# One core, gated-expert feed-forward on fp32 split in two: a bias load, one weight sum and one weight rest stand elsewhere in their queues

## The chip, the cores and the metric

One core of a Trainium2 chip. The metric is the device time of one execution in microseconds (us); 943.2 us is the median of three runs of the kernel before. One execution was also profiled, and all rows below come from it. 0.2% of the time is 1.9 us.

## The reference

```python
W = weights[condition]                      # one of 16 tables (64 x 64) for each of 128 batches
z = einsum('bct,bcd->bdt', x, W)
result = z @ W_base.T + b_base
logits = z @ W_gate.T                       # 8 experts
top_p, top_i = top_k(softmax(logits), 2)    # scaled to sum 1
h  = einsum('bnd,erd->bner', z, A)          # rank 16 for each of 8 experts
hw = h * route_w
out = x + result + einsum('bner,eor->bno', hw, B)
```

x has 128 batches of 64 rows and 1024 columns, so 8192 rows of 1024 fp32 values; all weights are fp32.

## The kernel before, in words

The order of the two linear maps is turned round: x is first multiplied by all weights (W_base, A and W_gate side by side, 1160 columns), which gives z; then `mix_chunk` (L829) multiplies z by the table of the batch. Every fp32 operand is split in two parts, hi (a copy rounded by ScalarE, functions `..._top`) and lo (whole minus hi, by VectorE or GpSimd, functions `..._rest`), and each product is three matmuls: hi·hi, hi·lo, lo·hi.

The 8192 rows are 64 tiles of 128, taken as 32 pairs of tiles, a and b (t = 0 and 1). The 1160 columns are three chunks: L (312 of W_base, the 128 of A, the 8 of W_gate: 448), Q (448) and R (264). From the third pair on, chunks L and Q of a pair are done by Strassen's scheme in seven products instead of eight. It needs sums of the weight blocks: T1 to T4, made once in `t_sum` (L614, VectorE), cut by `t_top` (L432, ScalarE) and `t_rest` (L618, VectorE). It also needs sums S1 to S4 of the halves of x^T, made for each pair by GpSimd (`sum_s1` to `sum_s4`, L322 to L347). The first pair and the second pair (function `first` of each engine, p = 1) are done with the weight blocks B11, B21, B12 and B22 themselves (`first_q`, L865), while the T's are made.

For each tile the rest goes: z is split (`z_top`, `z_rest`), mixed into banks ps_out that ScalarE has filled with the bias (`seed`, L443); from chunk L VectorE ranks the experts (`rank_experts`, L655), ScalarE takes one exponential (`exps`), VectorE makes hw (`weigh_experts`, L670). TensorE transposes hw (`turn_hw`, L838), hw is split (`hwt_top`, `hwt_rest`, L645) and multiplied by B (`lora`, L842) onto ps_out. VectorE adds x and the bank (`output`, L649), and SyncE's queue stores it.

The order on each engine is written out by hand, and semaphores tie the engines together. Four places matter here:

- SyncE's queue (from L218) issues the loads: x^T and weights in the order of need. `load_w` (L222) loads a weight block in two halves of 448 KB. The bias rows follow (L261 to L263), broadcast to 128 partitions. ScalarE copies the halves of B22 (`w_top`, L428) and then waits for all three bias loads before it seeds the banks.
- VectorE makes T1 and T3 right before its `first`, and T2 and T4 in it (L719 to L737), between work for tile b of the first pair (`hwt_rest(1)`, `output(0, 1, c)`) and tile a of the second.
- GpSimd in `first` (L382): it fetches the mixing tables (`fetch_mix`), makes S3 and S1 of the third pair, two a_lo (`a_rest`), then S2 and S4.
- TensorE's `first` (L949): `lora(1, c)` waits for hwt_lo; then mixing and lora of tile a; it ends with a wait for all four T rests (L982).

The queue of VectorE around the sums:

```python
            weigh_experts(0, 1)
            t_sum(1, T1, T3, T1)
            t_sum(3, T3, T2, T3)
            def first():
                z_rest(1, 0, L, ps_1[:, 0:NS])
                hwt_rest(1)
                t_sum(2, T2, T2, T1)
```

Of the kernel before, what the change touches and what calls it, by code (L numbers as in the profile page):

```python
# [13 lines left out]
P = 128  # L14
BANK = 512

BASE_COLS = [312, 448, 264]

L, Q, R = 0, 1, 2

B11, B21, B22, NT4, T1, T2, T3 = range(7)
# [9 lines left out]
def adaln_ffn(nc, x, x_t, cond, cond_w, w_t, b_t, b_base, out):  # L31
# [26 lines left out]
    at = [sum(width[:c]) for c in range(3)]  # L58
# [6 lines left out]
    with ExitStack() as ctx:  # L65
        def sb(name, shape, dt=F32):
            return ctx.enter_context(nc.sbuf_tensor(name, shape, dt))
# [10 lines left out]
        def sem(name):  # L78
            return ctx.enter_context(nc.semaphore(name))
# [10 lines left out]
        bias = sb("bias", [P, COLS])  # L90
# [43 lines left out]
        s_bias_in = sem("bias_in")  # L134
# [15 lines left out]
        s_w0_lo = {g: sem(f"{g}_lo_made") for g in ("B11", "B21", "B12", "B22")}  # L150
# [46 lines left out]
        def cols(c):  # L197
            return slice(at[c], at[c] + width[c])

        def base(c):  # L200
            return slice(base_at[c], base_at[c] + BASE_COLS[c])

        def ks(h):
            return slice(2 * h, 2 * h + 2)

        def as_f32(tile):
            return tile.bitcast(F32)

        def pairs(engine, first, step):
            first()  # L210
            with engine.Fori(2, PAIRS - 1) as p:
                step(p, False)
            step(PAIRS - 1, True)
# [3 lines left out]
        @block.sync  # L217
        def _(sp):  # L218
            w_src = w_t.rearrange("(k p) n -> p k n", p=P)
            home = {"B11": (T1, 0, L), "B21": (NT4, 1, L), "B12": (T3, 0, Q), "B22": (T2, 1, Q)}  # L220

            def load_w(g):  # L222
                at_g, half, c = home[g]
                for h in range(2):
                    sp.dma_start(w_sum[:, at_g, ks(h), :],
                                 w_src[:, half * KH + 2 * h:half * KH + 2 * h + 2, cols(c)]).then_inc(s_w_in[g][h], 16)

            def load_r(j):
                sp.dma_start(r_raw[:, ks(j), :], w_src[:, ks(j), cols(R)]).then_inc(s_r_in[j], 16)

            def load_raw(p, j):
                tile, half = 2 * p + j // 2, j % 2
                src = x_t[tile] if isinstance(tile, int) else \
                    x_t[bass.ds(tile, 1)].rearrange("a p k r -> (a p) k r")
                sp.dma_start(raw[j][:], src[:, half * KH:(half + 1) * KH, :]).then_inc(s_raw_in[j], 16)

            def load_x(p, t):
                sp.dma_start(o_sb[t][:], x[bass.ds((2 * p + t) * P, P), :]).then_inc(s_x_in[t], 16)

            def store(p, t):  # L240
                sp.wait_ge(s_out[t][(Q, R)[t]], p + 1)
                sp.dma_start(out[bass.ds((2 * p + t) * P, P), :], o_sb[t][:]).then_inc(s_stored[t], 16)

            load_raw(0, A11)
            load_r(0)
            load_raw(0, A21)
            load_r(1)
            load_w("B11")
            load_raw(0, A12)
            load_raw(0, A22)  # L250
            load_r(2)
            load_r(3)
            load_w("B21")
            for b in range(2):
                sp.dma_start(table_raw[b * C:(b + 1) * C], cond_w).then_inc(s_table_in, 16)
            load_w("B12")
            load_w("B22")
            for j in (A11, A21, A22):
                sp.wait_ge(s_a_lo[j], 1)
                load_raw(1, j)  # L260
            for c in range(3):  # L261
                sp.dma_start(bias[:, at[c]:at[c] + BASE_COLS[c]],
                             b_base[:, base(c)].to_broadcast([P, BASE_COLS[c]])).then_inc(s_bias_in, 16)  # L263
            sp.dma_start(b_raw[:], b_t).then_inc(s_b_in, 16)
            load_x(0, 0)
            sp.wait_ge(s_a_lo[A12], 1)
            load_raw(1, A12)
            load_x(0, 1)

            def step(p, last, first=False):  # L270
                if first:
                    sp.wait_ge(s_a_lo[A11], 2)
                elif not last:
                    sp.wait_ge(s_s_sum[2], p - 1)
                if not last:
                    load_raw(p + 1, A11)
                store(p - 1, 0)
                if not last:
                    sp.wait_ge(s_a_lo[A21], p + 1)
                    load_raw(p + 1, A21)  # L280
                    sp.wait_ge(s_a_lo[A22], p + 1)
                    load_raw(p + 1, A22)
                sp.wait_ge(s_stored[0], 16 * p)
                load_x(p, 0)
                if first:
                    sp.wait_ge(s_a_lo[A12], 2)
                elif not last:
                    sp.wait_ge(s_s_lo[4], p - 1)
                if not last:
                    load_raw(p + 1, A12)  # L290
                store(p - 1, 1)
                sp.wait_ge(s_stored[1], 16 * p)
                load_x(p, 1)

            pairs(sp, lambda: step(1, False, True), step)
            for t, c in ((0, L), (0, R), (0, Q), (1, L), (1, Q), (1, R)):
                sp.wait_ge(s_out[t][c], PAIRS)
                sp.dma_start(out[(TILES - 2 + t) * P:(TILES - 1 + t) * P, base(c)], o_sb[t][:, base(c)])\
                    .then_inc(s_stored[t], 16)
            sp.wait_ge(s_stored[0], 16 * (PAIRS + 2))  # L300
            sp.wait_ge(s_stored[1], 16 * (PAIRS + 2))
# [294 lines left out]
        def _(dve):  # L596
# [17 lines left out]
            def t_sum(t, to, one_at, other_at):  # L614
                dve.tensor_tensor(w_sum[:, to], w_sum[:, one_at], w_sum[:, other_at],  # L615
                                  ALU.subtract).then_inc(s_t_sum[t], 1)

            def t_rest(t, at_g):  # L618
                dve.wait_ge(s_t_hi[t], 1)
                dve.tensor_tensor(w_lo[:, at_g], w_sum[:, at_g], as_f32(w_hi[:, at_g]),  # L620
                                  ALU.subtract).then_inc(s_t_lo[t], 1)
# [23 lines left out]
            def hwt_rest(i, whole=ps_hwt[:, 0:P]):  # L645
                dve.wait_ge(s_hwt_hi, i + 1)
                dve.tensor_tensor(hwt_lo[:], whole, as_f32(hwt_hi[:]), ALU.subtract).then_inc(s_hwt_lo, 1)

            def output(p, t, c, bank=None):  # L649
                dve.wait_ge(s_x_in[t], 16 * p + 16)  # L650
                dve.wait_ge(s_out_mm[t][c], p + 1)
                dve.tensor_tensor(o_sb[t][:, base(c)], (bank or ps_out[c])[:, 0:BASE_COLS[c]], o_sb[t][:, base(c)],  # L652
                                  ALU.add).then_inc(s_out[t][c], 1)
# [65 lines left out]
            weigh_experts(0, 1)  # L719
            dve.wait_ge(s_w0_lo["B11"], 2)  # L720
            t_sum(1, T1, T3, T1)
            dve.wait_ge(s_w0_lo["B12"], 2)
            t_sum(3, T3, T2, T3)

            def first():
                z_rest(1, 0, L, ps_1[:, 0:NS])
                hwt_rest(1)
                dve.wait_ge(s_t_sum[1], 1)
                dve.wait_ge(s_t_sum[3], 1)
                dve.wait_ge(s_w0_lo["B22"], 2)  # L730
                t_sum(2, T2, T2, T1)
                for c in (L, Q, R):
                    output(0, 1, c)
                dve.wait_ge(s_t_sum[2], 1)
                dve.wait_ge(s_w0_lo["B21"], 2)
                t_sum(4, NT4, NT4, T2)
                rank_experts(1, 0)  # L737
                weigh_experts(1, 0)
                t_rest(1, T1)
                z_rest(1, 0, Q, ps_6[:, 0:NS])  # L740
                dve.wait_ge(s_t_sum[4], 1)
                t_rest(2, T2)
                z_rest(1, 0, R, ps_r[:, 0:width[R]])
                hwt_rest(2)
                dve.wait_ge(s_t_sum[3], 1)
                t_rest(3, T3)
                z_rest(1, 1, Q, ps_5[:, 0:NS])
                for c in (L, R, Q):
                    output(1, 0, c)
                t_rest(4, NT4)  # L750
                z_rest(1, 1, L, ps_1[:, 0:NS])
                z_rest(1, 1, R, ps_r[:, 0:width[R]])
                rank_experts(1, 1)
                weigh_experts(1, 1)
                turn_hw(3)
# [38 lines left out]
            def finish(p):  # L794
# [10 lines left out]
                output(p, 1, R)  # L805

            pairs(dve, first, step)

        @block.tensor
# [259 lines left out]
```

## Time and profile before

| | before |
|---|---|
| median of 3 runs (lowest to highest) | 943.2 us (943.04 to 944.24) |
| the profiled execution's own time | 942.72 us |
| its span (first to last instruction) | 941.0 us |
| TensorE matmuls busy | 935.8 us, 99% |
| VectorE busy | 525.5 us, 56% |
| GpSimd busy | 535.8 us, 57% |
| ScalarE busy | 384.4 us, 41% |
| granted TensorE clock | full in all slices |
| DMA, mean of the span | 114 GB/s |

The 1.7 us between own time and span lie outside the recorded instructions. A busy share is an average; which wait ends last at a place is read from the timeline there. Matmul rows of the timeline overlap: a matmul of 448 columns is listed with 0.36 us, and the next one starts 0.20 us after it. Missing time on TensorE is thus seen in the distance between starts.

### The profile page before, as it was taken

What the parts mean: (1) busy time and instruction counts of PE and PEld (TensorE: products, weight loads), DVE (VectorE), ACT (ScalarE), POOL (GpSimd) and SP (SyncE); (2) the same over time, 40 slices, a digit from 0 to 9 for tenths busy, and PEclk for the clock granted to TensorE, in tenths of its full rate; (3) what the DMA queues carried; (4) which work ended last, traced back from release to release, by engine and by line L of the source; (5) the groups of instructions that cost most, each with busy time, mean ns of one, the idle gap of its engine ahead of it and who ended that gap; (6) DMA issues with size and microseconds to landing.
All of it is one profiled execution on the core that took longest, in us unless ns stands there. A gap on an engine that the chain in (4) does not pass through costs nothing.

```text
span 941.0 us, 17296 instructions
## 1 busy us (share of the span) xinstructions
PE 935.8 (99%) x5444; PEld 880.9 (94%) x5444; DVE 525.5 (56%) x1808; ACT 384.4 (41%) x810; POOL 535.8 (57%) x506
## 2 busy tenths in 40 slices
PE   9999999999999999999999999999999999999998
PEld 7899999999999999999999999999999999999997
DVE  5785555545555455555555554555555555555554
ACT  6463343434334334444334344333443343434332
POOL 3575546655566555575555665555655547555560
PEclk9999999999999999999999999999999999999999
DMA  9522332233322233322333223333223332233312
GB/s 306 187 79 101 134 115 98 89 111 123 134 92 92 95 123 134 111 99 91 108 126 127 95 86 104 123 134 105 87 89 120 134 112 100 89 111 123 134 45 90
DMA packets 41453, 107.13 MB, mean 114 GB/s; under 512 B 4450, under 2 KB 8675, under 8 KB 41443
## 3 DMA queue, kind: packets, MB, share of 16 engines
q1 hardware_dynamic: 41440, 107.01, 32.9%
q8 instruction: 5, 0.08, 0.0%
q14 instruction: 6, 0.04, 0.0%
q10 hardware_dynamic: 2, 0.00, 0.0%
HBM read 73.43 MB, written 33.55 MB: 114 GB/s over the span
## 4 chain that ended last, share of the span: by engine, by line
PE 98%; DVE 1%; DMA 0%; ACT 0%; issue 0%; SPq 0%; DVEq 0%
PE ps L816 54%; PE ps_r L816 19%; PE ps_out L834 11%; PE ps_out L844 10%; PE ps L875 2%; PE ps L886 1%; DVE w_sum L615 1%; PE ps_r L875 1%; DMA raw<-in_x_t 0%; PE ps_hwt L840 0%; ACT a_hi L418 0%; PE ps_r L861 0%; PE ps L861 0%; PE ps L834 0%; DVE o_sb L652 0%; PE ps L844 0%
## 5 line engine op out<-in xcount | busy, mean ns | idle before, releaser
L316 POOL TENSOR_TENSOR a_lo<-raw,a_hi 128x512 fp32r<-128x512 f32 x128 | 165.9, 1318 | 245.1 <-ACT a_hi L418 245.1
L816 PE MATMUL ps<-w_hi,s_hi 128*128 128x448 f32 x480 | 177.6, 370 | 0.0
L816 PE MATMUL ps<-w_lo,s_hi 128*128 128x448 f32 x480 | 175.5, 366 | 0.0
L816 PE MATMUL ps<-w_hi,s_lo 128*128 128x448 f32 x480 | 173.6, 362 | 0.0
L632 DVE TENSOR_TENSOR z_sum<-ps,z_sum 128x448 f32<-128x448 f32 x150 | 93.7, 625 | 128.5 <-PE ps L816 128.3
L816 PE MATMUL ps_r<-r_hi,a_hi 128*128 128x264 f32 x496 | 140.7, 284 | 0.0
L816 PE MATMUL ps_r<-r_hi,a_lo 128*128 128x264 f32 x496 | 140.7, 284 | 0.0
L816 PE MATMUL ps_r<-r_lo,a_hi 128*128 128x264 f32 x496 | 140.6, 284 | 0.0
L652 DVE TENSOR_TENSOR o_sb<-ps_out,o_sb 128x312 f32<-128x312 f32 (+1 forms) x190 | 93.1, 505 | 76.8 <-PE ps_out L844 76.7
L816 PE MATMUL ps<-w_hi,a_hi 128*128 128x448 f32 x360 | 131.9, 367 | 0.0
L816 PE MATMUL ps<-w_hi,a_lo 128*128 128x448 f32 x360 | 130.6, 363 | 0.0
L816 PE MATMUL ps<-w_lo,a_hi 128*128 128x448 f32 x360 | 130.3, 362 | 0.0
L320 POOL TENSOR_TENSOR s_lo<-s_sum,s_hi 128x512 fp32r<-128x512 f32 x90 | 126.3, 1419 | 0.0
L834 PE MATMUL ps_out<-z_hi,mix 128*128 128x448 f32 (+1 forms) x380 | 120.9, 338 | 0.0
L446 ACT COPY ps_out<-bias 128x448 f32<-128x448 f32 (+1 forms) x190 | 90.0, 487 | 60.4 <-DVE o_sb L652 57.8
L642 DVE STREAM_TRANSPOSE hwt_sum<-hw 32x32 f32<-32x32 f32 x480 | 97.5, 203 | 15.1
L422 ACT CAST s_hi<-s_sum 128x512 fp32r<-128x512 f32 x90 | 55.7, 620 | 105.7 <-POOL s_sum L341 93.1
L816 PEld LDWEIGHTS ps<-w_hi,s_hi 128*128 128x128 f32 x480 | 90.0, 187 | 8.8
L816 PEld LDWEIGHTS ps<-w_hi,s_lo 128*128 128x128 f32 x480 | 90.0, 188 | 7.4
L816 PEld LDWEIGHTS ps<-w_lo,s_hi 128*128 128x128 f32 x480 | 90.2, 188 | 5.2
L816 PEld LDWEIGHTS ps_r<-r_lo,a_hi 128*128 128x128 f32 x496 | 93.4, 188 | 0.5
L816 PEld LDWEIGHTS ps_r<-r_hi,a_hi 128*128 128x128 f32 x496 | 93.2, 188 | 0.5
(135 smaller groups left out, 1711.3 us busy)
## 6 DMA issues: line engine op xcount, KB each, us to landing
raw<-in_x_t SPq DMA_DIRECT2D x128, 256.0 KB, 2.7
o_sb<-in_x SPq DMA_DIRECT2D x64, 512.0 KB, 3.6
out_x<-o_sb SPq DMA_DIRECT2D x62, 512.0 KB, 2.6
w_sum<-in_w_t SPq DMA_DIRECT2D x8, 448.0 KB, 9.2
r_raw<-in_w_t SPq DMA_DIRECT2D x4, 264.0 KB, 5.7
table_raw<-in_cond_w SPq DMA_DIRECT2D x2, 256.0 KB, 8.8
b_raw<-in_b_t SPq DMA_DIRECT2D x1, 512.0 KB, 10.8
out_x<-o_sb SPq DMA_DIRECT2D x2, 224.0 KB, 2.1
```

The costliest lines, as they stand in the source:

```text
L316: pool.tensor_tensor(a_lo[j][:], raw[j][:], as_f32(a_hi[j][:]), ALU.subtract).then_inc(s_a_lo[j], 1)
L320: pool.tensor_tensor(lo[:], whole, as_f32(hi[:]), ALU.subtract).then_inc(s_s_lo[j], 1)
L422: act.copy(hi[:], whole).then_inc(s_s_hi[j], 1)
L446: act.copy(ps_out[c][:, 0:width[c]], bias[:, cols(c)]).then_inc(s_seed[c], 1)
L615: dve.tensor_tensor(w_sum[:, to], w_sum[:, one_at], w_sum[:, other_at], ALU.subtract).then_inc(s_t_sum[t], 1)
L632: return dve.tensor_tensor(to, bank[:, 0:NS], other, ALU.add)
L642: dve.transpose(hwt_sum[c * TURN:(c + 1) * TURN, r * TURN:(r + 1) * TURN], hw[r * TURN:(r + 1) * TURN, c * TURN:(c + 1) * TURN]).then_inc( ...
L652: dve.tensor_tensor(o_sb[t][:, base(c)], (bank or ps_out[c])[:, 0:BASE_COLS[c]], o_sb[t][:, base(c)], ALU.add).then_inc(s_out[t][c], 1)
L816: mm = pe.matmul(bank[:, 0:w.shape[-1]], a[:, k, :], w[:, k, :], start=(opens and k == 0 and q == 0), stop=(closes and k == KH - 1 and q = ...
L834: mm = pe.matmul((bank or ps_out[c])[:, 0:width[c]], mix[t][:, m, :], z[t][:, cols(c)], start=False, stop=(q == 2), skip_group_check=True)
L844: mm = pe.matmul((bank or ps_out[c])[:, 0:BASE_COLS[c]], h[:], b[:, base(c)], start=False, stop=(q == 2), skip_group_check=True)
L875: mm = pe.matmul(bank[:, 0:NS], u[a][:, k, :], v[:, k, :], start=(half == 0 and k == 0 and q == 0), stop=(half == 1 and k == KH - 1 and q ...
```

## The change

SyncE's queue issues the three bias loads before the two loads of B22, not after them and the three loads of x^T. On VectorE the sum of T3 moves from in front of tile a's z_lo and tile b's hwt_lo to behind them; the three outputs of tile b now come before the sum of T2, and the rest of T1 is made after tile a's z_lo of chunks Q and R and its hwt_lo. Nothing is added or removed.

```diff
             load_w("B12")
+            for c in range(3):
+                sp.dma_start(bias[:, at[c]:at[c] + BASE_COLS[c]],
+                             b_base[:, base(c)].to_broadcast([P, BASE_COLS[c]])).then_inc(s_bias_in, 16)
             load_w("B22")
             for j in (A11, A21, A22):
                 sp.wait_ge(s_a_lo[j], 1)
                 load_raw(1, j)
-            for c in range(3):
-                sp.dma_start(bias[:, at[c]:at[c] + BASE_COLS[c]],
-                             b_base[:, base(c)].to_broadcast([P, BASE_COLS[c]])).then_inc(s_bias_in, 16)
@@
             t_sum(1, T1, T3, T1)
-            dve.wait_ge(s_w0_lo["B12"], 2)
-            t_sum(3, T3, T2, T3)
 
             def first():
                 z_rest(1, 0, L, ps_1[:, 0:NS])
                 hwt_rest(1)
+                dve.wait_ge(s_w0_lo["B12"], 2)
+                t_sum(3, T3, T2, T3)
+                for c in (L, Q, R):
+                    output(0, 1, c)
                 dve.wait_ge(s_t_sum[1], 1)
                 dve.wait_ge(s_t_sum[3], 1)
                 dve.wait_ge(s_w0_lo["B22"], 2)
                 t_sum(2, T2, T2, T1)
-                for c in (L, Q, R):
-                    output(0, 1, c)
                 dve.wait_ge(s_t_sum[2], 1)
                 dve.wait_ge(s_w0_lo["B21"], 2)
                 t_sum(4, NT4, NT4, T2)
                 rank_experts(1, 0)
                 weigh_experts(1, 0)
-                t_rest(1, T1)
                 z_rest(1, 0, Q, ps_6[:, 0:NS])
                 dve.wait_ge(s_t_sum[4], 1)
                 t_rest(2, T2)
                 z_rest(1, 0, R, ps_r[:, 0:width[R]])
                 hwt_rest(2)
+                t_rest(1, T1)
                 dve.wait_ge(s_t_sum[3], 1)
                 t_rest(3, T3)
                 z_rest(1, 1, Q, ps_5[:, 0:NS])
```

The queue of SyncE in the loads ahead of the first pair, as a difference (in_b_base is the bias, in_w_t the weights, raw the halves of x^T):

```order
 L255 DMA table_raw<-in_cond_w 64x1024 x2
-L225 DMA w_sum<-in_w_t 128x2x448 x4
+L225 DMA w_sum<-in_w_t 128x2x448 x2
+L258 DMA bias<-in_b_base 128x312
+L258 DMA bias<-in_b_base 128x448
+L258 DMA bias<-in_b_base 128x264
+L225 DMA w_sum<-in_w_t 128x2x448 x2
 L235 DMA raw<-in_x_t 128x512 x3
```

The bias stands between B12 and B22, ahead of two weight loads and three loads of x^T that it stood behind.

VectorE from tile b's hw of the first pair to the expert ranks of the second pair's tile a; L615 is a T sum, L625 a z_lo, L652 an output:

```order
 L682 SCALAR_TENSOR_TENSOR hw<-h_sb,e_inv,ps_hwt 128x128
-L615 TENSOR_TENSOR w_sum<-w_sum 128x1792 x2
+L615 TENSOR_TENSOR w_sum<-w_sum 128x1792
 L625 TENSOR_TENSOR z_lo<-ps,z_hi 128x448
 L647 TENSOR_TENSOR hwt_lo<-ps_hwt,hwt_hi 128x128
```

```order
 L652 TENSOR_TENSOR o_sb<-ps_out,o_sb 128x264
-L615 TENSOR_TENSOR w_sum<-w_sum 128x1792
+L615 TENSOR_TENSOR w_sum<-w_sum 128x1792 x2
 L659 COPY h_sb<-ps_out 128x64
```

One sum instead of two stands in front of z_lo and hwt_lo, one (T3) between hwt_lo and the outputs, and two (T2 and T4) in a row in front of the ranks.

VectorE behind tile a's hw; L620 is a T rest:

```order
 L682 SCALAR_TENSOR_TENSOR hw<-h_sb,e_inv,ps_hwt 128x128
-L620 TENSOR_TENSOR w_lo<-w_sum,w_hi 128x1792
 L625 TENSOR_TENSOR z_lo<-ps,z_hi 128x448
 L620 TENSOR_TENSOR w_lo<-w_sum,w_hi 128x1792
 L625 TENSOR_TENSOR z_lo<-ps_r,z_hi 128x264
 L647 TENSOR_TENSOR hwt_lo<-ps_hwt,hwt_hi 128x128
-L620 TENSOR_TENSOR w_lo<-w_sum,w_hi 128x1792
+L620 TENSOR_TENSOR w_lo<-w_sum,w_hi 128x1792 x2
 L625 TENSOR_TENSOR z_lo<-ps,z_hi 128x448
```

The z_lo of chunk Q follows hw at once, and two T rests (T1 and T3) now stand in a row behind hwt_lo.

## Rows read from the trace of the kernel before

**Rows 1.** The page, the chain that ended last, shares by engine.
```profile
PE 98%; DVE 1%; DMA 0%; ACT 0%; issue 0%; SPq 0%; DVEq 0%
```
**Rows 2.** Waits of PEld, whole span: line, waited for, total us, times, longest us.
```profile
PEld ps_out L834 <- issue: 0.4, 1, 0.4
PEld ps_out L834 <- DVE z_lo L625: 0.3, 1, 0.3
```
**Rows 3.** Timeline of PE at the first mixing: start, us, engine, line, op, out<-in, count.
```profile
26.89 0.37 PE L875 MATMUL ps_r<-w_hi,a_lo 128*128 128x448 f32 x1
27.29 0.44 PE L834 MATMUL ps_out<-z_hi,mix 128*128 128x448 f32 x1
```
**Rows 4.** Timeline of ACT; the idle time before and its releaser in brackets.
```profile
23.02 0.95 ACT L430 CAST w_hi<-w_sum 128x896 fp32r<-128x896 f32 x1
26.61 1.32 ACT L446 COPY ps_out<-bias 128x448 f32<-128x448 f32 x3 [2.64 <-DMA bias<-in_b_base]
...
41.95 0.53 ACT L437 CAST z_hi<-ps 128x448 fp32r<-128x448 f32 x1 [3.90 <-PE ps L875]
...
66.11 0.52 ACT L437 CAST z_hi<-ps 128x448 fp32r<-128x448 f32 x1
```
**Rows 5.** Issues of B22 on SP, their time to landing, and the stretch's DMA rate (last column).
```profile
10.19 1.16 SPq L225 DMA_DIRECT2D w_sum<-in_w_t  x2
...
DMA to landing us min/median/max: 11.1/11.7/12.2
...
20.00:27.00 7.00, 7.00 (x36) 6.37 (x34) 6.43 (x8) 4.09 (x6) 1.36 (x4) 1.00 1.05 389
```
**Rows 6.** Timeline of PE in the second pair, at lora of tile b.
```profile
44.09 0.36 PE L875 MATMUL ps<-w_hi,a_lo 128*128 128x448 f32 x1
44.64 0.41 PE L844 MATMUL ps_out<-b_hi,hwt_hi 128*128 128x312 f32 x1 [0.19 <-DVE hwt_lo L647]
```
**Rows 7.** Timeline of DVE: T sums (L615), hw (L682), z_lo (L625), a T rest (L620).
```profile
38.84 2.98 DVE L615 TENSOR_TENSOR w_sum<-w_sum 128x1792 f32<-128x1792 f32 x1
...
41.74 2.11 DVE L615 TENSOR_TENSOR w_sum<-w_sum 128x1792 f32<-128x1792 f32 x1
...
44.50 2.01 DVE L615 TENSOR_TENSOR w_sum<-w_sum 128x1792 f32<-128x1792 f32 x1
...
47.70 2.83 DVE L615 TENSOR_TENSOR w_sum<-w_sum 128x1792 f32<-128x1792 f32 x1
...
51.90 0.35 DVE L682 SCALAR_TENSOR_TENSOR hw<-h_sb,e_inv,ps_hwt 128x128 f32<-128x128 f32 x1
...
54.10 0.62 DVE L625 TENSOR_TENSOR z_lo<-ps,z_hi 128x448 fp32r<-128x448 f32 x1
...
60.84 2.57 DVE L620 TENSOR_TENSOR w_lo<-w_sum,w_hi 128x1792 fp32r<-128x1792 f32 x1
66.67 0.62 DVE L625 TENSOR_TENSOR z_lo<-ps,z_hi 128x448 fp32r<-128x448 f32 x1 [3.25 <-ACT z_hi L437]
```
**Rows 8.** Timeline of POOL: fetch (L354), S3, S1, two a_lo, S2 (L333).
```profile
39.88 2.08 POOL L354 CAST mix<-table 64x128 fp32r x1
...
47.36 1.29 POOL L341 TENSOR_TENSOR s_sum<-raw 128x512 f32<-128x512 f32 x1 [0.22 <-POOL mix L354]
48.61 3.07 POOL L327 TENSOR_TENSOR s_sum<-raw 128x512 f32<-128x512 f32 x1
...
57.43 4.10 POOL L316 TENSOR_TENSOR a_lo<-raw,a_hi 128x512 fp32r<-128x512 f32 x2 [5.74 <-ACT a_hi L418]
61.48 3.08 POOL L333 TENSOR_TENSOR s_sum<-s_sum,raw 128x512 f32<-128x512 f32 x1
```
**Rows 9.** Timeline of PE at tile a's transpose (L840) and its mixing behind.
```profile
54.50 0.27 PE L840 MATMUL ps_hwt<-ident,hw 128*128 128x128 f32 x1
54.77 0.47 PE L834 MATMUL ps_out<-z_hi,mix 128*128 128x448 f32 x1
```
**Rows 10.** Timeline of PE at tile b's mixing of chunk L.
```profile
67.44 0.38 PE L834 MATMUL ps_out<-z_hi,mix 128*128 128x448 f32 x1
```

## The prediction

> **What bounds the kernel now.** I read four views. The page's chain of work that ended last is TensorE for 98% of the span [rows 1], and no part of it waits in the repeated pairs. So only TensorE's own lost time counts, and the whole of it that this change can reach is in the first two pairs. The waits view names what feeds TensorE late: its weight loads for the mixing (L834) sat idle once for 0.4 us with no releaser named and once for 0.3 us behind z_lo [rows 2]. The timeline of TensorE gives the price of each place as the distance between starts: a matmul of 448 columns is followed 0.20 us later by the next. Three distances are too long:
>
> - A, first mixing: 26.89 to 27.29, so 0.20 us lost; the first matmul behind the hole takes 0.44 instead of 0.37, another 0.07 [rows 3].
> - B, lora of tile b: 44.09 to 44.64, so 0.35 us lost behind hwt_lo, and 0.41 against 0.31 in the same form for the matmul behind, 0.1 [rows 6].
> - C, mixing of tile a's chunk Q: the transpose at 54.50 normally costs 0.03, the mixing starts at 54.77, so 0.24 us lost [rows 9], and the z_lo that it needs ended at 54.72 [rows 7].
>
> Their sum is 0.27 + 0.45 + 0.24 = 0.96 us. That is the most that the change can give back, 0.10% of the time. A measurement of this kernel tells about 0.2% (1.9 us) from no change, once and for all below.
>
> **Part 1, bias ahead of B22.** ScalarE waits 2.64 us for the bias and seeds the banks from 26.61 [rows 4]; the first mixing needs the seed of chunk L, done some 0.5 us later, which is hole A. Six DMAs lie around it in SyncE's queue: three bias loads (512 KB together: 1024 columns of 4 bytes on 128 partitions) go ahead of two of B22, and with them ahead of three of x^T. Their bytes are the same and the DMA engines are saturated there, at 389 GB/s [rows 5], so bias arrives earlier by what it no longer stands behind (2 x 448 + 3 x 256 = 1664 KB, 4.4 us) and B22 later by 512 KB, 1.35 us. B22's second half was issued at 10.8 and landed 12.2 us later, at 23.0 [rows 5], and ScalarE copied it at 23.02 [rows 4]: it was just in time, so the delay is real. It now lands at 24.35; the copy (0.95) ends at 25.3; the seeds, which are queued behind that copy, start at 25.3 instead of 26.61, and chunk L is seeded at 25.8, 1.3 us ahead of TensorE at 27.1. The lo of that half takes VectorE at most 1.05 us (half of a T sum of 2.1, [rows 7]), so it is there at 26.4, and TensorE asks for it after 27.7. The x^T loads are 1.35 us later too, but their casts stand behind the seeds in ScalarE's queue, and the first of them is done for a product that TensorE starts past 35. So A goes, −0.27, and B22 costs nothing while its delay stays under about 2.6 us (seed ready at 27.1).
>
> **Part 2, T3's sum behind hwt_lo.** VectorE runs T1's and T3's sums from 38.84 to 43.85 [rows 7], while tile a's z_hi was ready at 42.48 (41.95 + 0.53, [rows 4]) and hwt_hi just behind. With one sum less in front, and everything 0.27 earlier, T1 ends at 41.55, VectorE then waits 0.65 us for z_hi until 42.2, and z_lo and hwt_lo (0.53 and 0.3 us from start to start of the next) are done by 43.0. TensorE asks at 44.0. B goes, −0.45. The three sums T3, T2, T4 (2.01 us each alone) with the outputs (1.3) between T3 and T2 follow.
>
> What this triggers is a collision with GpSimd. In the trace the two engines exclude each other when both read SBUF twice: T1's sum took 2.98 us, because it could only run once GpSimd's work ended at 39.88; the fetch of a small table took 2.08 us beside it [rows 8], and then T4's sum took 2.83 behind S3, and S1 3.07 us behind T4. I price it as "the later waits for the earlier, and who has waited longer goes next". T3 runs 43.0 to 45.0, the outputs to 46.25. S3 starts at about 45.35 and holds T2 until 46.65; T2 ends at 48.6. S1, which has waited since 46.65, goes next until 49.8; T4 ends at 51.8. Ranks and hw need 1.8 us as before (50.45 to 52.25): hw at 53.5, and z_lo of chunk Q right behind it at 54.1, because T1's rest (2.0 us) no longer stands between them. TensorE, 0.72 ahead, wants that z_lo at 54.77 − 0.24 − 0.72 = 53.8. So C does not go: it is 0.3 us long again, and the gain behind it is 54.77 − 54.1 = 0.67.
>
> The Trainium skill, "SBUF — State Buffer", section "Who interferes with whom", calls this an exclusive lock: a VectorE instruction with two SBUF inputs and a GpSimd instruction that reads SBUF block each other fully, and whoever issues first goes first. By a plain reading of it every one of T3, T2 and T4 may stand behind one GpSimd instruction of 1.3 us; this trace shows the blocking (2.98, 2.83, 3.07 us), and that case is the second rival.
>
> **Part 3, T1's rest behind hwt_lo(2).** T2's rest now runs 54.05 to 56.05, z_lo of chunk R and hwt_lo end at 56.6 (asked for at 57.2 and 57.6), T1's and T3's rests follow. Here GpSimd is queued too: its two a_lo took 4.10 us behind T3's rest, then S2 took 3.08 us, ending at 64.56, behind T4's rest (60.84, 2.57 us) [rows 7, 8]. S2's end matters: ScalarE cuts S2 and S1, seeds chunk L, and only then takes z_hi of tile b (66.11, 0.52) [rows 4], whose z_lo ends at 67.29 [rows 7], for the mixing at 67.44 [rows 10]. From S2's end to that mixing it is 2.88 us, with almost no slack. In the new order T1's rest ends at 58.5, one a_lo fits between it and T3's rest (59.75, 61.7), the other goes to 62.95, and S2 follows at once, as VectorE is then at its outputs (1.3 us, no second SBUF read) and reaches T4's rest only at about 63.4. S2 ends near 64.2, 0.35 earlier. The mixing then starts at 67.08 at best, 0.36 earlier than before, plus up to 0.1 of slack. T4's rest waits and ends at 66.1, and TensorE's wait for it comes past 67.
>
> **Sum.** −0.27 (A), −0.45 (B), nothing at C, and then about +0.2 at the last place: −0.5 us. From 943.2, the pairs behind being TensorE alone, that is 942.7. The profiled execution (942.72, 0.5 below the median) would become 942.2. The ends for the collision: none (−0.96), or every large VectorE step behind one GpSimd step.
>
> **Rivals.**
>
> 1. *All three holes close*: 942.2. If T4 follows T2 directly, hw is there at 52.3 and z_lo of Q at 53.0, ahead of 53.8; the T rests, the a_lo and S2 then all come 1 us earlier. Against it: the fetch of 39.88 ran as soon as T1 ended and T3 took 2.11 instead of 2.01, so a waiting GpSimd instruction does get in between [rows 7, 8].
> 2. *The collision eats the gain*: 943.1. Three waits of up to 0.8 us more on T3, T2 and T4 put z_lo of Q at 54.7, as late as now. For it: waits of that size are in the rows; against: VectorE's idle 0.65 us lets GpSimd's fetches through first.
> 3. *S2 misses its gap, slower*: the place is GpSimd's S2 beside T4's rest. If VectorE reaches T4's rest before the second a_lo is done (62.95, 0.45 us margin), T4 goes first for 2.0 us, S2 ends at 66.2, and tile b's mixing starts at 69.1 instead of 67.44: 944.8. It decides as soon as S2 ends later than 64.56.
> 4. *B22 late*: if the broadcast from one row moves far slower than 389 GB/s, at under 200 GB/s its delay passes 2.6 us and the seed is late again; at 129 GB/s the delay is 4 us and A costs 1.4 more than now forecast: 944.1. Against it: the DMA rate was at this level also while the bias was moving.
> 5. *The change does not act*: the bias wait may only change its name, as the seed stands behind B22's copy. That needs the delay of rival 4; with hole A kept and the rest as forecast it is 943.0.
>
> **Chances.** Forecast 0.45; all closed 0.17; eaten 0.15; S2 late 0.12; B22 late 0.03; bias wait kept 0.08. The range 941.9 to 944.1 reaches from rival 1, less 0.3 for the spread of runs (the lowest lay 0.16 below the median, the highest 1.04 above), to rival 4 and the smaller delays of rival 3. A gain beyond 1.9 us is twice what the rows allow: 0.02. A loss beyond it needs rival 3 with a second delay: 0.05. Within 0.2%: 0.93.
>
> **What would show it.** Right: no distance above 0.21 us at the first mixing, bias landing near 21.6 and B22 near 24.4; ScalarE's seeds at 25.3; lora of tile b without a wait; T2's or T4's sum at 2.4 to 3.2 us beside S3 and S1; T4's rest longer than 2 us, S2 short. Wrong: seeds still behind a bias wait; hw of tile a later than 54.2; S2 ending past 64.56; or any wait of TensorE in the repeated pairs, of which there should be none.

## The result, and the profile after

| | before | changed |
|---|---|---|
| median of 20 runs (lowest to highest) | 943.38 us (942.75 to 944.24) | 941.93 us (941.26 to 942.62) |
| profiled execution, own time | 942.72 us | 942.14 us |
| its span | 941.0 us | 940.4 us |

The ratio is 0.9984, 95% interval 0.9977 to 0.9990: 1.5 us faster (0.9 to 2.2), where 0.5 was forecast. That is below the 0.2% that the prediction took as the limit of "no change", and it is three times the forecast. The median lies at the very edge of the range (941.9); the ratio applied to the 943.2 from which the forecast started gives 941.7, just below it. The two profiled executions differ by 0.6 us only, and that was the first riddle.

TensorE's waits over the whole span of the changed kernel (line, waited for, total us, times, longest us):

```profile
PE ps_out L850 <- DVE zeros L597: 1.2, 1, 1.2
PE ps_r L886 <- ACT r_hi L426: 0.5, 1, 0.5
```

Both are in the first 8 us. Nothing is left of the waits behind hwt_lo and behind the bias. The timeline of TensorE in the changed kernel at the four places of the prediction (start, us, what):

```profile
27.20 0.36 PE L875 MATMUL ps_r<-w_hi,a_lo 128*128 128x448 f32 x1
27.40 0.37 PE L834 MATMUL ps_out<-z_hi,mix 128*128 128x448 f32 x1
...
44.24 0.36 PE L875 MATMUL ps<-w_hi,a_lo 128*128 128x448 f32 x1
44.44 0.31 PE L844 MATMUL ps_out<-b_hi,hwt_hi 128*128 128x312 f32 x1
...
54.20 0.27 PE L840 MATMUL ps_hwt<-ident,hw 128*128 128x128 f32 x1
54.24 0.47 PE L834 MATMUL ps_out<-z_hi,mix 128*128 128x448 f32 x1
...
66.90 0.37 PE L834 MATMUL ps_out<-z_hi,mix 128*128 128x448 f32 x1
```

They answer to [rows 3, 6, 9, 10]. Hole A is gone (0.20 between starts), hole B too, and so is hole C, which the prediction had kept: the mixing starts 0.04 behind the transpose, and the z_lo that it needs ended 0.05 before it, at 54.19 (below), so it closed with nothing to spare. The first matmul there still takes 0.47, 0.1 more than its like, as in [rows 9]. From 27.40 to 66.90 TensorE needs 39.50 us; before it was 27.29 to 67.44, 40.15.

VectorE in the changed kernel, the rows that answer to [rows 7]:

```profile
38.98 2.99 DVE L615 TENSOR_TENSOR w_sum<-w_sum 128x1792 f32<-128x1792 f32 x1
42.67 0.62 DVE L625 TENSOR_TENSOR z_lo<-ps,z_hi 128x448 fp32r<-128x448 f32 x1 [0.69 <-ACT z_hi L437]
43.21 0.28 DVE L647 TENSOR_TENSOR hwt_lo<-ps_hwt,hwt_hi 128x128 fp32r<-128x128 f32 x1
43.41 2.07 DVE L615 TENSOR_TENSOR w_sum<-w_sum 128x1792 f32<-128x1792 f32 x1
...
46.66 2.23 DVE L615 TENSOR_TENSOR w_sum<-w_sum 128x1792 f32<-128x1792 f32 x1
48.93 3.01 DVE L615 TENSOR_TENSOR w_sum<-w_sum 128x1792 f32<-128x1792 f32 x1
...
53.30 0.35 DVE L682 SCALAR_TENSOR_TENSOR hw<-h_sb,e_inv,ps_hwt 128x128 f32<-128x128 f32 x1
53.57 0.62 DVE L625 TENSOR_TENSOR z_lo<-ps,z_hi 128x448 fp32r<-128x448 f32 x1
...
63.34 2.57 DVE L620 TENSOR_TENSOR w_lo<-w_sum,w_hi 128x1792 fp32r<-128x1792 f32 x1
66.13 0.62 DVE L625 TENSOR_TENSOR z_lo<-ps,z_hi 128x448 fp32r<-128x448 f32 x1 [0.22 <-ACT z_hi L437]
```

and GpSimd, which answer to [rows 8]:

```profile
45.71 1.30 POOL L341 TENSOR_TENSOR s_sum<-raw 128x512 f32<-128x512 f32 x1
46.97 3.08 POOL L327 TENSOR_TENSOR s_sum<-raw 128x512 f32<-128x512 f32 x1
57.15 5.63 POOL L316 TENSOR_TENSOR a_lo<-raw,a_hi 128x512 fp32r<-128x512 f32 x2 [7.10 <-ACT a_hi L418]
62.74 1.28 POOL L333 TENSOR_TENSOR s_sum<-s_sum,raw 128x512 f32<-128x512 f32 x1
```

The idle 0.69 us of VectorE, T2 behind S3, S1 behind T2 (3.08 us), T4 behind S1 (3.01 us), T4's rest behind S2 (2.57 us) stand as drawn up in the prediction; T2 was hardly held up (2.23 us). hw is ready at 53.65 and S2 at 64.02; before it was 52.25 and 64.56.

ScalarE in the changed kernel at the loads, against [rows 4]:

```profile
24.42 0.94 ACT L430 CAST w_hi<-w_sum 128x896 fp32r<-128x896 f32 x1 [1.75 <-DMA w_sum<-in_w_t]
25.27 0.53 ACT L437 CAST z_hi<-ps 128x448 fp32r<-128x448 f32 x1
25.70 0.95 ACT L430 CAST w_hi<-w_sum 128x896 fp32r<-128x896 f32 x1
26.54 1.31 ACT L446 COPY ps_out<-bias 128x448 f32<-128x448 f32 x3
```

The seeds wait for no DMA. They start at 26.54, only 0.07 earlier than before and 1.2 us later than forecast, because the loads landed later than priced. The last bias load landed at 23.1 instead of 21.6, B22's first half at 24.4 instead of 22.7 (21.3 in the kernel before, and 1.35). The second half, whose copy stands in front of the seeds, landed at 25.6 instead of 24.35; it was issued at 12.3, and the last figure of this row is its time from issue to landing.

```profile
DMA to landing us min/median/max: 12.8/13.0/13.3
```

Part of the lateness is not the bias's: B12's second half, ahead of which nothing was moved, landed at 21.2 where it had been 20.2. It was just enough for TensorE. In the profiles of the kernel before, a first mixing that waits starts 0.68 us after the seeds; 26.54 and 0.68 are 27.22, and TensorE came at 27.40.

### The profile page after: what moved, and what is told of

Read it like the earlier page. It is cut to its first block, busy times and chain, and to the rows that moved or that the text cites. A ratio compares the mean times of both kernels' runs of the same rounds, so it can differ in the third digit from the quotient of the medians.

```text
span 940.4 us, 17296 instructions
## 1 busy us (share of the span) xinstructions
PE 935.2 (99%) x5444; PEld 881.0 (94%) x5444; DVE 526.9 (56%) x1808; ACT 383.9 (41%) x810; POOL 535.1 (57%) x506
## 4 chain that ended last, share of the span: by engine, by line
PE 99%; DMA 1%; SPq 0%; ACT 0%; DVE 0%; issue 0%; DVEq 0%
PE ps L816 54%; PE ps_r L816 19%; PE ps_out L834 11%; PE ps_out L844 9%; PE ps L875 3%; PE ps L886 1%; DMA r_raw<-in_w_t 1%; PE ps_r L875 1%; PE ps_hwt L840 0%; PE ps_r L861 0%; PE ps L861 0%; PE ps L834 0%; PE ps L844 0%; PE ps_r L886 0%; SPq L235 0%; ACT r_hi L426 0%
## 5 line engine op out<-in xcount | busy, mean ns | idle before, releaser
L652 DVE TENSOR_TENSOR o_sb<-ps_out,o_sb 128x312 f32<-128x312 f32 (+1 forms) x190 | 93.1, 505 | 76.9 <-PE ps_out L844 76.8
L834 PE MATMUL ps_out<-z_hi,mix 128*128 128x448 f32 (+1 forms) x380 | 120.8, 338 | 0.0
```

Source lines behind the costliest of these rows:

```text
L834: mm = pe.matmul((bank or ps_out[c])[:, 0:width[c]], mix[t][:, m, :], z[t][:, cols(c)], start=False, stop=(q == 2), skip_group_check=True)
```

## The experiments

Each was timed beside runs of the kernel before on the same chip, and profiled once. The intervals of a single comparison are about 0.9 us to each side, wider than most of the effects. So each profile is read too, in two numbers: when the first mixing (L834) starts, and the own time minus that start.

| kernel | median us | ratio (95%) | own time | first mixing | own minus first mixing |
|---|---|---|---|---|---|
| before, first profile | 943.38 | | 942.72 | 27.29 | 915.43 |
| e1 before again | 943.28 | 0.9999 (0.9990 to 1.0008) | 943.45 | 27.94 | 915.51 |
| e2 bias alone | 942.53 | 0.9991 (0.9982 to 1.0000) | 942.79 | 27.33 | 915.46 |
| e3 T3 and outputs alone | 944.46 | 1.0014 (1.0005 to 1.0023) | 944.33 | 27.66 | 916.67 |
| e4 T3, outputs and T1's rest | 942.57 | 0.9993 (0.9984 to 1.0002) | 943.22 | 28.60 | 914.62 |
| changed, first profile | 941.93 | 0.9984 (0.9977 to 0.9990) | 942.14 | 27.40 | 914.74 |
| e5 changed again | 941.96 | 0.9987 (0.9978 to 0.9996) | 941.96 | 27.30 | 914.66 |
| e6 T1's rest alone | 942.99 | 0.9997 (0.9988 to 1.0006) | 942.84 | 27.84 | 915.00 |
| e7 bias later | 945.78 | 1.0024 (1.0015 to 1.0033) | 946.47 | 29.66 | 916.81 |
| e8 e3 with GpSimd held back | 945.25 | 1.0022 (1.0013 to 1.0032) | 944.84 | 27.57 | 917.27 |
| e9 bias ahead of B12 | 942.98 | 0.9996 (0.9987 to 1.0005) | 943.17 | 28.44 | 914.73 |
| e10 changed, one load by ScalarE | 941.32 | 0.9978 (0.9969 to 0.9987) | 941.64 | 26.76 | 914.88 |
| e11 changed, two loads by ScalarE | 941.13 | 0.9978 (0.9968 to 0.9987) | 941.23 | 26.85 | 914.38 |
| e12 before, two loads by ScalarE | 942.21 | 0.9986 (0.9977 to 0.9995) | 942.62 | 27.56 | 915.06 |

**e1, the kernel before once more.**

> The kernel before itself, for a second profile and as the null of the comparison. Theory H (three holes of fixed size): the ratio is 1.000 and the profile shows the same distances as the first one, 0.20 us lost at the first mixing, 0.35 at lora of tile b, 0.24 at tile a's mixing of Q. Theory V (the holes vary from execution to execution, and the first profile was a favourable one, 0.7 us under the median): this profile shows more lost time, 0.3 to 0.8 us, at the first mixing or in the first 10 us, in an execution that is longer by as much.

The ratio is 1. The profile is the one that answers the riddle. ScalarE's seeds, and TensorE at the first mixing:

```profile
27.26 1.31 ACT L446 COPY ps_out<-bias 128x448 f32<-128x448 f32 x3 [2.48 <-DMA bias<-in_b_base]
```

```profile
26.88 0.37 PE L875 MATMUL ps_r<-w_hi,a_lo 128*128 128x448 f32 x1
27.94 0.44 PE L834 MATMUL ps_out<-z_hi,mix 128*128 128x448 f32 x1 [0.70 <-ACT ps_out L446]
```

The hole is 0.86 us, not 0.20; TensorE was as early as in the first profile (26.88 against 26.89), the bias landed 0.65 us later. Behind the first mixing the two executions agree within 0.08 us. Theory V holds here.

**e2, the bias alone** (the SyncE part of the diff shown above, nothing else).

> Only the bias loads move ahead of B22. Theory H: 0.27 us faster than before. Theory V (the bias often lands later than in the first profile, so that the first hole is larger in the median than the 0.20 us seen): 0.6 to 0.9 us faster. Both: the seeds no longer wait for the bias, and no hole at the first mixing.

0.69 us faster by the medians (942.53 against 943.22), as theory V has it; the interval (0 to 1.7 us) includes H's 0.27 as well. The own time behind the first mixing is 915.46, unchanged, so the whole effect lies ahead of it. In this profile the usual 0.20 us stands between the last B12 product and the mixing:

```profile
27.13 0.36 PE L875 MATMUL ps_r<-w_hi,a_lo 128*128 128x448 f32 x1
27.33 0.37 PE L834 MATMUL ps_out<-z_hi,mix 128*128 128x448 f32 x1
```

**e3, T3's sum and the outputs alone.**

```diff
             t_sum(1, T1, T3, T1)
-            t_sum(3, T3, T2, T3)
...
                 hwt_rest(1)
+                t_sum(3, T3, T2, T3)
+                for c in (L, Q, R):
+                    output(0, 1, c)
                 t_sum(2, T2, T2, T1)
-                for c in (L, Q, R):
-                    output(0, 1, c)
```

> Only T3's sum and the outputs move (T1's rest stays ahead of z_lo of chunk Q, the bias stays behind B22). Theory H with the order of VectorE: the hole at lora closes (0.45 us), but hw of tile a comes about 1.3 us later, T1's rest (2.0 us) follows it, and z_lo of Q is ready near 56.1 where TensorE wants it at 54.1: 0.9 to 1.3 us slower than before, all of it lost at tile a's mixing of Q. Rival (VectorE's later order has slack everywhere): 0.45 us faster.

1.24 us slower, as theory H with the order of VectorE said. Hole B is closed, and hole C has grown to 2.0 us:

```profile
54.43 0.27 PE L840 MATMUL ps_hwt<-ident,hw 128*128 128x128 f32 x1
56.44 0.47 PE L834 MATMUL ps_out<-z_hi,mix 128*128 128x448 f32 x1 [1.74 <-DVE z_lo L625]
```

So T3's move by itself is a loss. It pays only with T1's rest out of the way of z_lo.

**e4, T3's sum, outputs and T1's rest, no bias.**

> T3's sum, the outputs and T1's rest move, the bias does not. Theory H: 0.7 us faster (0.45 at lora, 0.24 at tile a's mixing of Q), the 0.2 us hole at the first mixing stays. Theory V: the rest of the measured 1.5 us lies in the bias, so here too 0.7; if it lies in the VectorE part, 1.2.

0.65 us faster (942.57 against 943.22), near the 0.7 of both theories and not the 1.2 that would have put the surplus into VectorE's part. In this profile TensorE reached the first mixing at 28.60, 1.3 us later than in the first profile, and did not wait there: the seeds had started at 26.88. That it began the x product at 6.38 instead of 5.35 does not explain it, since e2 began at 6.68 and was at the first mixing at 27.33. What differs is the pace behind the begin. Until about 10.3 us the matmuls of 264 columns start 0.22 us apart (a row of two covers 0.44), in e2 0.12:

```profile
7.84 0.64 PE L886 MATMUL ps<-r_hi,a_hi 128*128 128x264 f32 x2
8.28 0.64 PE L886 MATMUL ps<-r_lo,a_hi 128*128 128x264 f32 x2
```

The granted clock of this trace is listed as 1.00 there, so it does not show why. Behind the first mixing the execution needed 914.62 us, 0.8 less than before. So VectorE's part is worth 0.8 behind the first mixing, B and C together.

**e5, the changed kernel once more.**

> The changed kernel itself, for a second profile. Both theories: 1.3 to 1.6 us faster than before. Theory V (in the kernel before the first mixing waits for the bias's landing, so its time does not depend on when TensorE began; in the changed one it does not wait): no hole at the first mixing, and the time of the first mixing minus the time at which the B12 products begin is 4.9 us whenever TensorE began.

1.34 us faster. The two profiles agree at 27.30 and 27.40, and at 914.66 and 914.74. From the first B12 product (22.44 and 22.46) to the mixing it is 4.86 and 4.94 us, the theory's 4.9.

**e6, T1's rest alone.**

```diff
                 weigh_experts(1, 0)
-                t_rest(1, T1)
                 z_rest(1, 0, Q, ps_6[:, 0:NS])
...
                 hwt_rest(2)
+                t_rest(1, T1)
```

> Only T1's rest moves behind hwt_lo of tile a. Hole at tile a's mixing of Q closes: 0.24 us faster; S2 ends near 63.3 in the time of the first profile, so nothing is lost at tile b's mixing of L. Rival (two T rests in a row beside GpSimd's two a_lo push S2 past 64.6): up to 1.5 us slower, with a hole in front of tile b's mixing of L.

0.31 us faster by the medians, not told from nothing by its interval. In the profile hole C is closed and the hole at lora stays; 915.00 behind the first mixing is 0.5 less than before. No hole opened at tile b's mixing of L (0.12 between starts); the rival falls.

**e7, the bias one load further back.**

```diff
             sp.dma_start(b_raw[:], b_t).then_inc(s_b_in, 16)
+            for c in range(3):
+                sp.dma_start(bias[:, at[c]:at[c] + BASE_COLS[c]], ...).then_inc(s_bias_in, 16)
```

(and away from its place ahead of the load of B's matrix)

> The bias loads go one place further back, behind the 512 KB load of B's matrix. Theory V: the bias lands 1.35 us later (512 KB at 389 GB/s), the seeds and the first mixing with it, and the whole 1.35 us is lost: 1.2 to 1.4 us slower than before, hole at the first mixing 1.6 to 2.2 us. Theory H, in which only a hole of 0.2 us stands there and something else gave the rest: less than 1 us.

2.5 us slower, twice what was expected. The hole at the first mixing is 2.6 us, and behind it came something else. TensorE, and the windows around it (busy times of the engines, then the granted clock, DMA share, GB/s):

```profile
26.83 0.37 PE L875 MATMUL ps_r<-w_hi,a_lo 128*128 128x448 f32 x1
29.66 0.71 PE L834 MATMUL ps_out<-z_hi,mix 128*128 128x448 f32 x1 [2.45 <-ACT ps_out L446]
...
30.91 0.57 PE L875 MATMUL ps<-w_hi,a_hi 128*128 128x448 f32 x1
31.29 0.57 PE L875 MATMUL ps<-w_lo,a_hi 128*128 128x448 f32 x1
...
33.45 0.37 PE L875 MATMUL ps<-w_hi,a_lo 128*128 128x448 f32 x1
33.65 0.36 PE L875 MATMUL ps<-w_hi,a_hi 128*128 128x448 f32 x1
```

```profile
20.00:27.00 7.00, 7.00 (x36) 6.34 (x34) 6.36 (x8) 4.08 (x6) 1.11 (x3) 1.00 1.06 385
27.00:29.60 2.60, 0.20 (x1) 0.00 (x0) 0.14 (x2) 0.63 (x2) 0.50 (x2) 0.97 0.99 386
29.60:33.00 3.40, 3.35 (x9) 3.03 (x10) 1.78 (x8) 2.47 (x5) 0.56 (x1) 0.52 0.12 47
33.00:40.00 7.00, 7.00 (x39) 6.46 (x39) 3.71 (x12) 2.67 (x6) 2.73 (x2) 1.00 0.11 37
```

After 2.6 us without a matmul the granted clock is 0.52 from 29.6 to 33.0: the 1.2 GHz level, starts 0.37 us apart instead of 0.20. Nine matmuls at 0.17 each cost 1.5 us more, near the difference of 916.81 to 915.46 behind the first mixing (1.35). The later first mixing gives 29.66 - 27.9 = 1.8 us, where 27.9 is the first mixing that the median of the kernel before implies (worked out below). Together that is 3.1 us for the profiled execution, which was 0.7 longer than the median. The runs lie apart (944.2 to 947.0); whether those near 944.5 kept the full clock was not profiled.

**e8, e3 with GpSimd held back.**

```diff
+                pool.wait_ge(s_z_lo[0][Q], 2)
                 sum_s3(2, True)
                 sum_s1(2, True)
```

> As the run in which only T3's sum and the outputs moved, and GpSimd's sums S3 and S1 of the third pair wait until z_lo of tile a's chunk Q is made. If the collision of T2's and T4's sums with S3 and S1 was what made hw late, T2 and T4 take 2.0 us each, hw comes 1.6 us earlier, and the hole of 1.98 us at tile a's mixing of Q shrinks to 0.3 to 0.5: 1.5 us faster than that run, 0.3 faster than before. If the order of VectorE's queue alone made it late, nothing changes against that run (1.2 us slower than before).

The total missed both expectations: 1.95 us slower than before (945.25 against 943.30), where 0.3 faster or 1.2 slower was expected. Still the profile tells them apart. T2's and T4's sums take 4.07 us together, where in e3 they took 5.27, and the hole at tile a's mixing of Q falls from 1.98 to 0.72 us. So 1.2 us of e3's hole was the collision with GpSimd. What was gained was lost later, and more, and this is where rival 3 of the prediction shows itself: S3 and S1 now stand in the way of the two a_lo, S2 ends at 66.71, and tile b's mixing of L follows 2.79 us behind it.

```profile
65.43 1.28 POOL L333 TENSOR_TENSOR s_sum<-s_sum,raw 128x512 f32<-128x512 f32 x1
```

```profile
67.65 0.29 PE L817 MATMUL ps_r<-r_hi,a_lo 128*128 128x264 f32 x1
69.50 0.47 PE L835 MATMUL ps_out<-z_hi,mix 128*128 128x448 f32 x1 [1.56 <-DVE z_lo L626]
```

The path from S2's end to that mixing, 2.88 us in the prediction, is real (2.79 here).

**e9, the bias ahead of B12 too** (changed kernel, the three bias loads one block further ahead).

> The changed kernel with the bias one step further ahead, in front of B12. Theory V (the bias needs only to land ahead of TensorE's first mixing, and every load in front of it is late by 1.35 us): B12 lands near 20.3 and 21.5 instead of 19.0 and 20.2, its lo is ready near 22.4 where TensorE wants it at 22.2 and 22.8 to 23.8 for the second half, so 0.3 to 1.2 us slower than the changed kernel. Rival (the earlier the better): as fast as the changed kernel or faster.

1.0 us slower than the changed kernel by the medians (942.98 against 941.96 in e5), inside the expected 0.3 to 1.2 (the two were timed on different chips; their differences to the kernel before, 0.28 and 1.34, give the same). B12 is what is late now:

```profile
22.14 0.37 PE L875 MATMUL ps<-w_hi,a_lo 128*128 128x448 f32 x1
23.21 0.44 PE L875 MATMUL ps<-w_hi,a_hi 128*128 128x448 f32 x1 [0.71 <-DVE w_hi L608]
```

Of the two loads that the bias was put ahead of, B22 has slack and B12 has none.

**e10 and e11, the start.** With nothing left to wait for at the first mixing, the changed kernel's time should depend on the first 8 us, where its last wait ends. The edit of e11, against the changed kernel (e10 has it for `load_r(0)` alone, and leaves the load of the table numbers where it is):

```diff
-            load_r(0)
...
-            load_r(1)
...
+            for j in range(2):
+                act.dma_start(r_raw[:, ks(j), :], w_act[:, ks(j), cols(R)]).then_inc(s_r_in[j], 16)
```

> The changed kernel with the first load of chunk R's weights issued from ScalarE's queue beside SyncE's first load. If the changed kernel's time is set by the loads of the first 8 us, and those by the rate at which SyncE issues them (0.45 us each), TensorE begins and goes on 0.3 to 0.5 us earlier and the whole is 0.3 to 0.5 us faster than the changed kernel. If the DMA engines' rate sets them, nothing changes (0.1).

> As the run before, but both first loads of chunk R's weights come from ScalarE's queue, and the load of the table numbers goes behind its first exponential. By issue rate: 0.4 to 0.8 us faster than the changed kernel. By the DMA engines' rate: no change, or slower where the x^T loads and the weights share the engines and both land later.

e10 is 0.6 us faster than the changed kernel (941.32 against 941.96 in e5, on another chip; somewhat over the 0.3 to 0.5), e11 0.8 (941.13), inside the 0.4 to 0.8 that the rate of issue gave. SyncE issues its first loads of the changed kernel 0.46 us apart, and in e11 two engines issue at once:

```profile
0.80 0.40 SPq L235 DMA_DIRECT2D raw<-in_x_t  x1
1.26 0.41 SPq L229 DMA_DIRECT2D r_raw<-in_w_t  x1
```

```profile
0.79 1.00 ACTq L412 DMA_DIRECT2D r_raw<-in_w_t  x2
```

Everything behind is issued and lands earlier, and the first mixing starts at 26.76 and 26.85 instead of 27.3. e11 is the fastest kernel here: ratio 0.9978 (0.9968 to 0.9987) to the kernel before, 2.1 us, and its 10 runs lie within 0.2 us (941.06 to 941.26), where those of the kernel before, 26 on the same chip, are spread over 1.8.

**e12, the kernel before with e11's start.**

> The kernel BEFORE (bias behind B22, sums as they were) with the first loads of chunk R's weights issued from ScalarE's queue. In the changed kernel that edit gave 0.8 us. Theory V (before, the first mixing waits for the landing of the bias, whatever TensorE did until then): an earlier begin of TensorE only makes the hole at the first mixing longer; the time falls by no more than the bias lands earlier, 0 to 0.3 us against before, and the hole is 0.5 us or longer. Theory H (a small hole of 0.2 us): 0.6 to 0.8 us faster than before, less 0.2.

0.94 us faster. Theory V, at most 0.3, missed; theory H, 0.4 to 0.6, missed too, but by less. The profile has what V asked for: TensorE earlier (26.57), a hole of 0.79 us, the seeds waiting for the bias until 26.88.

```profile
26.88 1.31 ACT L447 COPY ps_out<-bias 128x448 f32<-128x448 f32 x3 [2.50 <-DMA bias<-in_b_base]
```

```profile
26.57 0.37 PE L876 MATMUL ps_r<-w_hi,a_lo 128*128 128x448 f32 x1
27.56 0.44 PE L835 MATMUL ps_out<-z_hi,mix 128*128 128x448 f32 x1 [0.62 <-ACT ps_out L447]
```

But the profiled execution (942.62) is the slowest of its 11 runs; the median, less the 915.06, puts the first mixing at 27.15, so the start's edit probably brings the bias in earlier too, by more than the 0.3 that V allowed. No profile shows that. And 0.4 us of the difference lies behind the last matmul: own time minus its start is 5.04 here and 5.44 in the kernel before. That is not clearly the edit's work. It is 5.11 in e11, but 5.62 in e10, and 5.28 to 5.48 in the eleven profiles with the old start. The 11 runs here also lie within 0.6 us, where the kernel before beside them is spread over 2.8; so part of the spread probably belongs to the start.

## Why the prediction was wrong, and where it was right

**The step that failed first is A's size.** "So A goes, −0.27" took the hole from one profile, 0.20 us plus 0.07. In six profiles TensorE waited at the first mixing with the bias load in its old place (before, e1, e3, e6, e8, e12), and in all six the first mixing follows the seeds by 0.68 us: seeds at 26.61, 27.26, 26.98, 27.16, 26.89, 26.88, mixing at 27.29, 27.94, 27.66, 27.84, 27.57, 27.56. In these the landing decides, and the first profile had the earliest of the six. (In e4, the seventh with the bias there, the seeds started at 26.88 and TensorE itself was later, at 28.60.)

Behind the mixing the kernel before needs 915.46 us (915.43 and 915.51), so its median of 943.38 means a first mixing at 27.9. For the changed kernel it is 941.93 - 914.70 = 27.2. The difference, 0.7 us, is what e2 measured (0.69). The same subtraction, median less the time behind the mixing in the one profile, is an estimate for every kernel: 27.8 to 28.0 in all with bias and start as they were (e1, e3, e4, e6, e8), and 27.1 in e2 and 27.3 in e5 with the bias ahead of B22. TensorE's late arrival, seen once in e4, can fall on either kind alike and does not explain that difference. The text had noted that the profiled execution lay 0.5 us below the median, and carried these 0.5 us along as if they lay outside the argument. They lay for the most part in the very hole that the change closes.

**The second is C and what followed from it.** "So C does not go: it is 0.3 us long again" came out of a long chain that put T4's end at 51.8. Shifted by the 0.41 us by which this execution's T1 rows and those of the working differ (it reached the first mixing at 27.40 where the working had 27.1, and hole A's 0.27 is already taken off there), the measured T4 ended at 51.5, S1 at 49.6 and z_lo at 53.8, just when TensorE asked. Each step of the chain was right in kind, S3 before T2, S1 before T4, and the whole was 0.3 us too long. Instructions that follow each other overlap by 0.05 to 0.1 us in the rows (T3 starts at 43.41, hwt_lo at 43.21 takes 0.28), and the working had added up durations; that this is the whole of the 0.3 us was not tried. With C open the last place was also priced at a loss of 0.2; it cost nothing, since S2 was ready 0.5 us earlier than before. B came as priced: 0.45. B and C together gave 0.76 behind the first mixing (915.46 to 914.70), and 0.65 by the medians of e4, where the prediction left 0.25.

**Right:**

- TensorE loses nothing in the repeated pairs: no wait of it there, in any profile.
- The bias delays B22 by about its bytes over the rate, 1.35 us. Counted from the landing of B12, B22's second half lands 2.8 to 3.1 us later in before, e1, e3, e4, e6, e7 and e8, and 4.3 to 4.6 us later in e2, e5 and the changed kernel's first profile.
- B22 has the slack for it. The first mixing came 0.9 and 0.7 us after the seed could have released it in e2 and e5, and 0.2 in the changed kernel's first profile, where B12 was 1.0 us late as well.
- T3's sum needs T1's rest out of the way (e3).
- VectorE and GpSimd hold each other up (e8; T4 3.01 and S1 3.08 us).

**The rivals.** Rival 1, all three holes close, is what happened; its gain of 0.96 was still 0.5 short of the 1.45 between the medians, mostly for A's size. Rival 2 falls: the collision cost about 1.2 us on VectorE (e8 against e3), and z_lo still ended 0.05 us before its mixing. Rival 3's mechanism is real, and was seen with another edit (e8), not here: S2 was 0.5 us earlier, not later. Rivals 4 and 5 fall: the bias did not move far slower than the rest, and no seed waited for it. The direction of the price in rival 4 was still right, as e9 shows for B12.

On the rule of the Trainium skill, "SBUF — State Buffer", section "Who interferes with whom": the rows agree with full blocking (S1 3.08 us beside T2's and before T4's sum, 1.3 alone). What decided here is who goes next at a release. In the rows it is each time the one already waiting: S1 behind T2, then T4 behind S1, as the prediction had it.

**Open**: what makes the bias land so differently that the seeds start between 26.6 and 27.3 from execution to execution; why B12 landed 1.0 us later in the changed kernel's first profile than in that of the kernel before, and why B22's first half is delayed more than its second (counted from B12, it landed after 3.1 to 3.4 us with the bias ahead of it, 1.1 to 1.9 without); why TensorE ran at about half its pace until 10.3 us in e4; and why the time behind the last matmul is 5.0 to 5.6 us.

## What to carry to other kernels

When a hole on the bounding engine ends with a DMA's landing, its size in a profile is that of one execution. Profile the same kernel twice, and ask where the difference between the profiled time and the median lies. Compare executions by the time left behind a fixed instruction, which here agreed within 0.1 us where totals were spread over 1.5. A change made of several moves in the queues is worth testing move by move: one of these loses 1.2 us alone and gains with its neighbour.

## What the runs showed of the hardware

- A hole of 2.6 us on TensorE was followed by a granted clock of 0.52 in the stretch read behind it (29.6 to 33.0) and cost 1.35 us on top (e7); holes of 2.0 us (e3), of 0.9 and of 1.7 us (e6, e8) were followed by full clock.
- Where VectorE and GpSimd held each other up, the one already waiting at the release went next: S3, T2, S1, T4 in this order in the changed kernel, each ending 1.2 us (GpSimd) or 1.9 us (VectorE) behind the other's end.
- Issuing one or both of the first weight loads from ScalarE's queue beside SyncE's gave 0.6 to 0.9 us (e10, e11, e12) in a kernel of 940, though the DMA rate in the stretch from 2 to 6 us did not rise (272 GB/s in the changed kernel, 268 in e11); from 6 to 10 us it was 359 and 393.
- 512 KB put ahead of a load in one busy queue (about 380 GB/s) made it land 1.2 to 1.8 us later, counted from the load in front of both, where 512 KB over 389 GB/s are 1.35 us.
